# Second expert layer: the token weights are made by replacing the kept exponentials in the row of 32, in place of an index lookup and a table of 8 picks by 32 experts

## What is computed

```python
logits = x @ gate_weight.T                          # 1024 x 32
probs = softmax(logits)
topv, topi = top_k(probs, 8)
topv = topv / clip(topv.sum(-1), 1e-12)
scaled = topv * layer_alpha
active = scaled >= 0.05                             # where none is: the largest alone
routing_weights = topv * active
routing_weights = routing_weights / clip(routing_weights.sum(-1), 1e-12)
combine = zeros((1024, 32)).at[token, topi].add(routing_weights)
for e in range(32):                                 # every expert on every token
    g, u = split(x @ gate_up[e].T)
    out += (silu(g) * u) @ down[e].T * combine[:, e]
```

## Time and profile before

| | |
|---|---|
| median of 3 runs | 645.79 us (644.98 to 646.8) |
| the profiled execution's own time | 648.34 us |
| its span in the profile | 646.5 us |
| mean granted TensorE clock | 0.918 of full speed |
| TensorE busy | 545.7 us, 84% |
| VectorE busy | 329.2 us, 51% |
| GpSimd busy | 353.0 us, 55% |
| ScalarE busy | 224.3 us, 35% |

### The profile page before, as it was taken

The page is one execution under the profiler, slowest core; times in us unless marked ns, Lnnn a source line. Parts: engine busy times, 40 slices in busy tenths (PEclk is TensorE's granted clock), DMA queues, the critical chain, the costliest instruction groups (busy, mean ns, idle before and its releaser), DMA issues.

```text
span 646.5 us, 9617 instructions
## 1 busy us (share of the span) xinstructions
PE 545.7 (84%) x3085; PEld 445.6 (69%) x3085; DVE 329.2 (51%) x726; ACT 224.3 (35%) x526; POOL 353.0 (55%) x316
## 2 busy tenths in 40 slices
PE   8899865149999996639898877797999999999995
PEld 4666664138888885628664435785888888888885
DVE  4645786504665432212379895667333323335365
ACT  4645442104555763312350201432222222222233
POOL 3473115777578886550027876016484585759190
PEclk9979997578999997768898996998999999999999
DMA  8999882334667665430000006100333423423221
GB/s 258 374 386 386 286 271 74 108 121 120 190 201 220 207 183 175 119 97 24 0 1 1 1 0 189 31 2 7 106 93 98 146 99 98 122 79 115 61 65 66
DMA packets 72866, 83.71 MB, mean 129 GB/s; under 512 B 7618, under 2 KB 63699, under 8 KB 72819
## 3 DMA queue, kind: packets, MB, share of 16 engines
q1 hardware_dynamic: 33490, 38.90, 19.9%
q10 hardware_dynamic: 35968, 35.26, 16.3%
q0 software_dynamic: 3360, 8.93, 4.4%
HBM read 48.61 MB, written 34.47 MB: 128 GB/s over the span
## 4 chain that ended last, share of the span: by engine, by line
PE 63%; DVE 13%; issue 7%; DMA 4%; ACT 2%; another core or an unknown queue 2%; ACTq 1%; POOL 0%; DVEq 0%
PE PS L1841 45%; DMA FA<-xg 4%; PE PS L2065 2%; DVE FA L1797 2%; DVE PS L1779 2%; PE PS L2183 2%; PE PS L2207 1%; PE PS L2294 1%; PE PS L1916 1%; PE PS L1938 1%; PE PS L2108 1%; PE PS L2078 1%; PE PS L2306 1%; DVE HC L1553 1%
## 5 line engine op out<-in xcount | busy, mean ns | idle before, releaser
L1841 PE MATMUL PS<-XH,EW 128*128 128x512 f32 x400 | 133.2, 398 | 0.1
L1841 PEld LDWEIGHTS PS<-XH,EW 128*128 128x128 f32 x400 | 76.0, 190 | 16.6 <-DVE EW L1200 0.6
L1569 DVE TENSOR_TENSOR FA<-OGATE,PS 128x512 f32<-128x512 f32 x42 | 28.9, 688 | 110.8 <-ACT OGATE L1008 94.6
L1841 PE MATMUL PS<-EW,XH 128*128 (+2 forms) x252 | 79.8, 401 | 6.1 <-issue 4.7
L1841 PE MATMUL PS<-XL,EW 128*128 128x512 f32 x200 | 79.1, 396 | 0.0
L1008 ACT ACTIVATE OGATE<-PS 128x512 f32<-128x512 f32 x48 | 28.7, 599 | 127.8 <-PE PS L1841 127.8
L801 POOL TENSOR_TENSOR FA<-FA,QT 128x1024 f32<-128x1024 f32 (+1 forms) x16 | 37.5, 2342 | 61.2 <-DVE FA L1797 61.2
L1841 PE MATMUL PS<-EW 128*128 128x256 f32 x288 | 62.8, 283 | 0.5 <-DVE W1L L1574 0.4
L1841 PE MATMUL PS<-EW,W1L 128*128 128x256 f32 x192 | 54.3, 283 | 0.0
L1841 PEld LDWEIGHTS PS<-EW,XH 128*128 128x128 f32 x252 | 46.3, 204 | 11.3 <-issue 5.6
L1841 PEld LDWEIGHTS PS<-EW 128*128 128x128 f32 x288 | 49.4, 190 | 4.0 <-DVE W1L L1574 1.2
(11 more groups left out here) (385 smaller groups left out, 1278.9 us busy)
## 6 DMA issues: line engine op xcount, KB each, us to landing
xg<-EQ ACTq DMA_DIRECT2D x1, 16384.0 KB, 61.0
EG<-in_gateup SPq DMA_DIRECT2D x16, 448.0 KB, 4.0
yg<-EQ ACTq DMA_DIRECT2D x1, 6016.0 KB, 20.3
FA<-xg ACTq DMA_DIRECT2D x47, 128.0 KB
yg<-FA ACTq DMA_DIRECT2D x47, 128.0 KB, 1.9
ED<-in_down SPq DMA_DIRECT2D x16, 224.0 KB, 4.7
EG<-in_gateup SPq DMA_DIRECT2D x16, 192.0 KB
FA<-in_gateup SPq DMA_DIRECT2D x16, 192.0 KB, 3.0
```

The lines of the kernel that those rows point to most:

```text
L1569: dve.tensor_tensor(mixed[:, i % MIXED, :], sil_t[:, i % 2, :], bank(step_bank(i) + 1), ALU.mult).then_inc(mixed_dve, 1)
L1841: ins = pe.matmul(o, l, r, start=start and i == 0, stop=stop and i == n - 1, skip_group_check=True)
```

## The change

In `softmax` the index lookups, their cast to floats and the division of the 8 by the row's sum go. In their place the 8 exponentials are summed, the sum is floored by 1e-12 times the row's sum into rv, and the 8 are multiplied by the reciprocal into t1. `route1` starts from there, and its last line masks the exponentials themselves (top) in place of the normalised picks. `combine` no longer builds a table. For each tile, `match_replace` writes the row of 32 with each element that equals one of the 8 kept exponentials replaced by -1 (`marked`; picks that are dropped are zero there). Between them the inverse of the kept sum is made. One pass over 128 x 256 compares with -1 and multiplies by the exponentials, and one scales the row into CW. `marked` lies at the start of HC, where the table lay. The last normalisation and its semaphore wait go.

```diff
--- before.py
+++ after.py
@@ -269,7 +269,7 @@
         mixed = FA[:, KD * QUAD * 2 * I1:KD * QUAD * 2 * I1 + MIXED * BANK].rearrange("p (s c) -> p s c", s=MIXED)
         sil_t = OGATE[:].rearrange("p t d -> p (t d)")[:, 0:2 * BANK].rearrange("p (s c) -> p s c", s=2)
         up_t = OGATE[:].rearrange("p t d -> p (t d)")[:, 2 * BANK:4 * BANK].rearrange("p (s c) -> p s c", s=2)
-        hot = HC[:].rearrange("p t d -> p (t d)")[:, 0:NT * E1 // 2 * 8].rearrange("p (t e k) -> p t e k", t=NT, k=8)
+        marked = HC[:].rearrange("p t d -> p (t d)")[:, 0:NT * E1].rearrange("p (t e) -> p t e", t=NT)
         spread_w = [HC[:].rearrange("p t d -> p (t d)")[:, 2 * BANK:3 * BANK],
                     HC[:].rearrange("p t d -> p (t d)")[:, 3 * BANK:4 * BANK], QT[:, 0:BANK], QT[:, BANK:2 * BANK]]
         cw_turned = flat(WW[:])[0:E1, 0:T]
@@ -1505,17 +1505,14 @@
                 for t in range(NT):
                     ins = dve.max(top[:, t, :], PR[:, t, 0:E])
                 largest = ch.mark(ins)
-                summed = ch.mark(dve.tensor_reduce(rsum[:], pr, AX_X, ALU.add))
+                ch.link(dve.tensor_reduce(rsum[:], pr, AX_X, ALU.add))
                 ch.need(largest)
-                for t in range(NT):
-                    ins = dve.max_index(tix[:, t, :], top[:, t, :], PR[:, t, 0:E])
-                found = ch.mark(ins)
-                ch.need(summed)
-                inverse = ch.mark(dve.reciprocal(rsum[:], rsum[:]))
-                ch.need(found)
-                dve.tensor_copy(tif[:], tix[:])
-                ch.need(inverse)
-                ch.link(dve.tensor_tensor(top[:], top[:], col(rsum[:], 8), ALU.mult))
+                ch.link(dve.tensor_reduce(rbest[:], top[:], AX_X, ALU.add))
+
+                ch.link(dve.scalar_tensor_tensor(out=rv[:], in0=rsum[:], scalar=1e-12, in1=rbest[:], op0=ALU.mult,
+                                                 op1=ALU.max))
+                ch.link(dve.reciprocal(rsum[:], rv[:]))
+                ch.link(dve.tensor_tensor(t1[:], top[:], col(rsum[:], 8), ALU.mult))
 
             def normalise(dst, src, k, floor):
 
@@ -1527,8 +1524,7 @@
 
             def route1():
 
-                ch.link(normalise(t1, top, 8, 1e-12))
-                ch.link(dve.tensor_scalar(t2[:], t1[:], alpha[:, 0:1], None, ALU.mult))
+                ch.link(dve.tensor_tensor(t2[:], t1[:], alpha[:, 0:1].unsqueeze(2).broadcast_to([P, NT, 8]), ALU.mult))
                 ch.link(dve.tensor_reduce(rsum[:], t2[:], AX_X, ALU.max))
                 ch.link(dve.tensor_tensor(t3[:], t2[:], col(rsum[:], 8), ALU.is_equal))
                 f8 = first8[:].unsqueeze(1).broadcast_to([P, NT, 8])
@@ -1540,21 +1536,25 @@
                 ch.link(dve.tensor_tensor(t3[:], f8, col(rbest[:], 8), ALU.is_equal))
                 ch.link(dve.scalar_tensor_tensor(out=t2[:], in0=t2[:], scalar=TAU, in1=t3[:], op0=ALU.is_ge,
                                                  op1=ALU.max))
-                ch.link(dve.tensor_tensor(t1[:], t1[:], t2[:], ALU.mult))
+                ch.link(dve.tensor_tensor(t1[:], top[:], t2[:], ALU.mult))
 
             def combine():
 
 
-                shape = [P, NT, E1 // 2, 8]
-                each = lambda x: x.unsqueeze(2).broadcast_to(shape)
-                for e0 in (0, E1 // 2):
-                    ch.link(dve.tensor_tensor(hot, iota_e[:, e0:e0 + E1 // 2].unsqueeze(1).unsqueeze(3).broadcast_to(shape),
-                                              each(tif[:]), ALU.is_equal))
-                    ch.link(dve.tensor_tensor(hot, hot, each(t2[:]), ALU.mult))
-                    ins = dve.tensor_reduce(CW[:, :, e0:e0 + E1 // 2], hot, AX_X, ALU.add)
-                    if e0 == 0:
-                        ch.link(ins)
-                ins.then_inc(cw_step, 1)
+                kept = ch.mark(dve.tensor_reduce(rsum[:], t1[:], AX_X, ALU.add))
+                for t in range(NT):
+                    ins = dve.match_replace(marked[:, t, :], t1[:, t, :], PR[:, t, :], -1.0)
+                    if t == 0:
+                        ch.need(kept)
+                        floored = ch.mark(dve.scalar_tensor_tensor(out=rsum[:], in0=rv[:], scalar=1e-12, in1=rsum[:],
+                                                                   op0=ALU.mult, op1=ALU.max))
+                    if t == 2:
+                        ch.need(floored)
+                        dve.reciprocal(rsum[:], rsum[:])
+                ch.link(ins)
+                ch.link(dve.scalar_tensor_tensor(out=CW[:], in0=marked, scalar=-1.0, in1=PR[:], op0=ALU.is_equal,
+                                                 op1=ALU.mult))
+                dve.tensor_tensor(CW[:], CW[:], col(rsum[:], E1), ALU.mult).then_inc(cw_step, 1)
 
             def moe_dve():
 
@@ -1823,8 +1823,6 @@
             lo_parts(3, XL, XH)
             softmax(1, E1)
             route1()
-            normalise(t2, t1, 8, 1e-12).then_inc(weights_ready, 1)
-            dve.wait_ge(weights_ready, 2)
             combine()
             moe_dve()
             layernorm_halves(3, XA)
```

## The result

| | before | changed |
|---|---|---|
| median of 22 runs | 646.67 us | 643.21 us |
| ratio, with its 95% interval | | 0.9948 (0.9925 to 0.9971) |
| profiled execution, its span | 648.34, 646.5 us | 640.31, 638.5 us |

The change is faster by 0.5%: 3.4 us, 1.9 to 4.9. I had forecast 639.5 in 637.9 to 641.9, a gain of 6.3 or 1.0%. The median lies outside, on the slow side.

What follows compares the result with a forecast made beforehand. TensorE was taken to stall on VectorE's chain into CW; 4.69 us idle plus 0.62 and 0.95 us of low clock made 6.3 us, taken off the median 645.79 for 639.5 us, range 637.9 to 641.9.

Steps and rivals of the forecast that it cites:

- What bounds the kernel: Second router: TensorE's transposes of the combine weights wait for VectorE's chain into CW, 4.69 us idle.
- The new chain: VectorE's shortened chain into CW ends at 439.3 us, bounds 436.9 and 441.5; replace pairs 0.16 us each, two links held.
- What could be late next: After the stall goes: ScalarE's copy of step 5's up half, free by 1.4 us; weights' way through DRAM, about 2 us left.
- The sum: TensorE, stall to first down matmul: 4.69 us idle, 0.62 in transposes, 0.95 in steps 6 to 10, together 6.3 us.
- The claimed floor of 4.7 us: Lower bound of the gain: TensorE's idle time before the transposes alone, if the clock falls anyway.
- theory A: Follow-up theory: the traces are typical and the measured gain is scatter about 6.3 us.
- Rival 2: Clock still falls around the transposes, or first down matmul waits about 1 us for weights: gain 4.7 to 5.3; chance 0.10.
- Rival 1: Part of the stall before the transposes stays because replace pairs are slow: gain 2.7 to 4.3 us; chance 0.07.
- Rival 3: Replace pairs so slow that VectorE's chain ends later than today: 651 us at 2 us each; chance 0.02.
- Rival 4: No effect: something else holds TensorE at 444.07, or GpSimd gives the gain back late: 645 to 646 us; chance 0.03.

Runs made afterwards that it cites:

- its two edited forms: The kernel before with 26 idle matmuls in TensorE's layer norm wait: 0.9988 of the kernel before; and with expert step 3's 12 matmuls issued twice: 0.9975.
- N = 8: Changed kernel with eight idle VectorE reductions ahead of the replacement, so the weights are ready about as late as before: 1.0018 of the kernel before.
- N = 3: Changed kernel with three idle VectorE reductions ahead of the replacement: 0.9909 of the kernel before.
- the doubled pair: Kernel before and changed kernel, each with expert step 3's 12 matmuls issued twice: 0.9975 and 0.9989 of the kernel before.
- the doubled kernel before: The kernel before with the 12 matmuls of expert step 3 issued twice: 0.9975 of the kernel before.
- the broken one: Changed kernel with expert step 0 put between router tiles 0 to 3 and 4 to 7: 0.9951 of the kernel before.
- N = 24: Changed kernel with 24 idle VectorE reductions ahead of the replacement: 1.0325 of the kernel before, with a traced stall of 22.4 us.

## Why the prediction was wrong

**What bounds the kernel**: right. The transposes waited for CW, and nothing behind them took the time back.

**The new chain**: right, and close. CW was ready 9.1 us after the first maximum, where the forecast of 439.3 meant 9.7. The replace pair cost 0.16 us, the value taken; the two holds by GpSimd's multiplies fell on the two links named. The Trainium skill (SBUF — State Buffer, the section on its two separate sides) says that the port pair which VectorE and GpSimd share is an exclusive lock, for which a VectorE instruction contends when it has two SBUF inputs and the GpSimd instruction reads SBUF, or when it runs in a 2-port mode. The new rows agree: the one-input reduction at 432.36 ran its 0.22 us across GpSimd's start at 432.41, and the two-input comparison at 432.61 was held. The number of inputs alone doesn't decide, though: in the kernel before, two one-input `tensor_scalar` passes took 0.89 us (128x8, L1524) and 1.18 us (128x64, L1531) beside GpSimd's multiplies, and the 128x8 one 0.17 us away from them. None of that had a bearing on the time, since the slack was 5 us.

**What could be late next**: right in both places. The weights' way through DRAM, from the copy at 443.69 to the weighting at 449.65, was even shorter, 5.96 us against 8.13.

**The sum**: this failed, at "so I take the same 6.3 off the median". The three terms (4.69 idle, 0.62 and 0.95 of low clock) hold for the traced pair, where they came out as 4.68, 0.68 and 0.94. None of them is a constant of the kernel. The idle time is the difference between two paths: VectorE's chain, which is nearly fixed (24.5 to 25.5 us from the first router matmul in the kernel before, its two edited forms and N = 8), and TensorE's steps 0 to 5, which take 16.8 us, 18.1 with a low stretch of 3.4 us, and 19.6 with one of 6.8. I had called steps 0 to 5 the cover of the chain, and taken the cover's length from one execution in which nothing slowed it. The claimed floor of 4.7 us for the gain was no floor: with a low stretch of 3.4 us in the cover the idle time was 3.5 us (N = 8), and the clock behind it held. So the step that failed is the idle term and its clock terms taken as the same in every execution: forecast 6.3 us, measured 3.4 (1.9 to 4.9). The evidence that a single trace was thin ground stood in the same trace, where the clock was 0.50 from 418.2 to 421.6 us with TensorE busy throughout, 5.7 us before the cover begins.

From the stage table an average can be estimated. The changed kernel's five traces (the N = 3 one among them) have a mean of (35.3 + 38.5 + 36.9 + 36.9 + 35.3)/5 = 36.6; the kernel before and its likeness with N = 8 have (41.6 + 40.7)/2 = 41.2. That makes 4.6 us, from two traces on one side. The four comparisons of the changed kernel with the kernel before gave ratios of 0.9948, 0.9892, 0.9920 and 0.9970; weighted by their intervals 0.9946, within 0.0016, so about 3.5 us, 2.4 to 4.5. That, and the doubled pair, exclude theory A's fixed 6.3. By these few traces the low stretch explains some 1.7 of the 2.8 us by which the forecast was too high. Whether the last one is scatter (seven traces are few), a cost of the change outside the wait (the doubled pair leaves room for up to 1.9) or something that no trace showed stays open.

**Rival 2**, "the clock falls around the transposes all the same", was the nearest in size but put the loss in the wrong place. The clock falls 19 to 20 us before the transposes, and not in the changed kernel alone: it also fell under the wait of N = 8 and of the doubled kernel before, and the wait hid it. Rivals 1, 3 and 4 did not happen.

**What was shown and what was argued.** Shown: that the stall hides slow work of TensorE under it (the doubled step), and that the clock does fall there in seven of ten traces. Shown within 2 us at best: that of the change only the time at which CW is ready counts (the doubled pair; N = 3 and N = 8 within 3 to 4). Filling the layer norm's wait goes with a steady clock in four traces of four with the whole router, and in one of two with the broken one. How much of the shortfall the low stretch explains is an estimate from seven traces. Why the clock falls behind the router is not shown. With the whole router and idle matmuls some 10 us ahead of it the low stretch never came, and with dense matmuls in the router's middle it still did. So an unbroken run of 32 narrow matmuls is neither enough for it nor needed.

**The version that beats both** is the changed kernel with the 26 idle matmuls: 0.9907, 0.9869 and 0.9918 of the kernel before on three chips, and 3.4 and 3.8 us below the changed kernel on the two chips that had both. The traces account for some 2.5 us of that. Half of it comes from the stretch right behind the layer norm: from the transposes to the first router matmul it takes 5.1 us with the fill, and on average 6.3 in the changed kernel's five traces without (6.5 to 6.8 in four, 5.1 in the one whose clock fell only at the router's end). The other half is the mean stage of 36.6 us against 35.3. Where the rest comes from is not shown. It uses nothing that the kernel doesn't hold, but it runs TensorE for no result.

## What to carry to other kernels

A stall is the gap between two chains. Before its length from one trace is booked as a gain, ask what varies under it: with the stall gone, every delay of the engine that used to wait counts in full, and the average gain can be less than the traced gap. Look for stretches elsewhere in the trace where that engine's clock falls, since such a stretch may lie in the cover in the next execution. Removing a wait also changes what the next edit is worth: idle matmuls in an earlier wait gave the old kernel 0.8 us, within its noise, and the new one 3.4.

## What was not expected of the hardware

The granted clock fell in TensorE's busy time, not only in or right behind idle time: with the 3.4 us wait 8 to 10 us past and TensorE busy since (in six of seven traces the clock had fallen there too, and come back), it went to half at the router's end and stayed there for 3.4 us (six traces) or 6.8 us (one), while 512-column matmuls were running back to back. And the same changed kernel showed it in three executions and not in a fourth. Around a stall of 3.5 to 4.7 us it fell for 3.4 us (two traces) or 6.8 us (one), and in one (N = 8) not at all. In the 22.4 us stall of N = 24 it fell 5.3 us into the idle time and was back at full 3.3 us behind it.
